# Gated cross-attention with a sign-weight FFN on one core: the first stage with x loaded from ScalarE's queue, weights alone in SyncE's and rounded one unit ahead

## The reference

```python
x = x + tanh(g_xattn) * attention(layernorm(x), ctx, ctx, mask, wq, wk, wv, wo)
x = x + tanh(g_ffn) * ffn(layernorm(x), weight, bias, gate_w, in_channel_scale, out_channel_scale)
```

## Time and profile before

| | us |
|---|---|
| median of three runs | 1526.08 |
| lowest and highest | 1522.46, 1531.22 |
| the profiled execution | 1529.2 |
| its span | 1527.4 |
| first matmul of the first stage | 14.40 |
| first matmul of the next stage | 90.44 |

### The profile page before, as it was taken

One profiled execution on the slowest core, in us unless ns is written; L12 is line 12 of the kernel. 1 busy time (PEld: TensorE's weight loads), 2 busy tenths in 40 slices (PEclk: granted clock), 3 DMA queues, 4 the chain that ended last, 5 costly groups with the idle time before them and its releaser, 6 DMA issues.

```text
span 1527.4 us, 26067 instructions
## 1 busy us (share of the span) xinstructions
PE 1483.2 (97%) x8720; PEld 1311.3 (86%) x8720; DVE 1031.4 (68%) x2373; ACT 615.2 (40%) x1183; POOL 722.8 (47%) x594
## 2 busy tenths in 40 slices
PE   5989999999999999999999998999999999989998
PEld 5878888888888888888888788999999999978887
DVE  5837888888778888888788874455455455765653
ACT  5732222222222222222222364556567565634442
POOL 6834445654555546555455452333333333335554
PEclk9999999999999999999999999999999999999999
DMA  7830222212221222212221686443997442542311
GB/s 271 289 110 27 71 77 69 69 48 69 76 76 48 76 69 76 69 41 76 73 79 42 194 332 219 133 130 100 374 392 226 132 131 96 187 144 106 110 69 69
DMA packets 95210, 192.56 MB, mean 126 GB/s; under 512 B 9056, under 2 KB 36192, under 8 KB 95008
## 3 DMA queue, kind: packets, MB, share of 16 engines
q1 hardware_dynamic: 88944, 179.74, 36.2%
q10 hardware_dynamic: 6192, 11.86, 2.3%
HBM read 133.90 MB, written 57.67 MB: 125 GB/s over the span
## 4 chain that ended last, share of the span: by engine, by line
PE 85%; issue 3%; POOL 2%; DVE 2%; DMA 1%; ACT 1%; SPq 0%; POOLq 0%; ACTq 0%; DVEq 0%
PE bank L52 19%; PE bank L53 19%; PE bank L54 19%; PE bank L915 7%; PE bank L914 7%; PE bank L916 7%; PE bank L937 5%; POOL last_rows L1352 1%; DMA w_raw<-in_wo 1%; PE bank L950 1%; DVE project L1504 1%; ACT project L1130 1%; POOL feed L1344 0%; PE bank L959 0%; PE bank L982 0%
## 5 line engine op out<-in xcount | busy, mean ns | idle before, releaser
L52 PE MATMUL bank<-x_hi,w_hi 128*128 128x512 f32 x1024 | 399.2, 390 | 3.9 <-PEq L67 3.9
L53 PE MATMUL bank<-x_lo,w_hi 128*128 128x512 f32 x1024 | 398.9, 390 | 0.0
L54 PE MATMUL bank<-x_hi,w_lo 128*128 128x512 f32 x1024 | 398.8, 389 | 0.0
L1504 DVE TENSOR_TENSOR project<-bank,project 64x256 fp32r<-64x256 f32 x512 | 216.1, 422 | 197.4 <-ACT project L1130 192.0
L1357 POOL TENSOR_TENSOR w_lo<-w_raw,w_hi 128x512 fp32r<-128x512 f32 x128 | 165.7, 1296 | 285.7 <-ACT w_hi L1122 285.7
L1130 ACT CAST project<-bank 64x256 fp32r<-64x256 f32 x512 | 188.4, 368 | 160.6 <-PE bank L54 150.6
L1291 POOL TENSOR_TENSOR q_lo<-rot,q_hi 128x512 fp32r<-128x512 f32 x128 | 164.9, 1293 | 184.7 <-ACT q_hi L1061 184.6
L915 PE MATMUL bank<-project,project 128*128 128x256 f32 x832 | 235.8, 283 | 0.0
L914 PE MATMUL bank<-project,project 128*128 128x256 f32 x832 | 235.8, 283 | 0.0
L916 PE MATMUL bank<-project,project 128*128 128x256 f32 x832 | 235.8, 283 | 0.0
L52 PEld LDWEIGHTS bank<-x_hi,w_hi 128*128 128x128 f32 x1024 | 192.6, 188 | 44.2 <-issue 4.1
(11 more groups left out here) (143 smaller groups left out, 2696.7 us busy)
## 6 DMA issues: line engine op xcount, KB each, us to landing
w_raw<-in_wo SPq DMA_DIRECT2D x128, 256.0 KB, 3.0
project<-probs_scratch SPq DMA_DIRECT2D x52, 512.0 KB, 8.7
w_raw<-in_wq SPq DMA_DIRECT2D x32, 512.0 KB, 5.3
probs_scratch<-pt_hi SPq DMA_DIRECT2D x64, 256.0 KB, 2.6
probs_scratch<-pt_lo SPq DMA_DIRECT2D x64, 256.0 KB, 3.2
x_in<-in_x SPq DMA_DIRECT2D x16, 512.0 KB, 4.9
last_rows<-in_x SPq DMA_DIRECT2D x8, 1024.0 KB, 6.2
x_scratch<-last_rows SPq DMA_DIRECT2D x8, 1024.0 KB, 5.6
```

Source lines behind the costliest of these rows:

```text
L52: pe.matmul(out, hi, rhs_hi, start=first, stop=False, **kw)
L53: pe.matmul(out, hi, rhs_lo, start=False, stop=False, **kw)
L54: return pe.matmul(out, lo, rhs_hi, start=False, stop=last, **kw)
L1504: done = nc.vector.tensor_tensor(vw_lo[i][at], vw_ps[hp % VW_BANKS][b * SK:(b + 1) * SK, h, :], vw_hi[i][at].bitcast(F32), ALU.subtract)
```

## The change

Five edits, all in `prepare`:

1. SyncE loads both halves of ctx and units 0 and 1 first, and then tiles 0 to 2 of x. The later tiles are loaded from ScalarE's queue, each right behind the normalisation that frees its buffer.
2. SyncE's queue then holds only the weights and, in ScalarE's place, the stores of keys and values: from step 6 every second step behind the load of a unit, from step 14 each step.
3. ScalarE rounds unit `n + 1` in step `n`. Unit 0 is rounded between the two halves of ctx.
4. GpSimd takes the deviation of tile `n` behind the low part of unit `n` (tiles 0 and 1 both behind unit 1).
5. VectorE takes ctx_lo before the statistics of tile 0.

The waits for the last stores stand on SyncE instead of ScalarE.

```diff
@@ sync
-            def load_x(i):
-                wait(sp, xn_ready, i - XB + 1)
-                sp.dma_start(x_in[:, i % XB], a["x"][i * P:(i + 1) * P, :]).then_inc(x_in_sem[i % XB], 16)
+            def store_keys(gp):
...
+            def store_values(g):
...
             for h in range(2):
                 src = a["ctx_t"].rearrange("(k p) t -> p k t", p=P)[:, half(h)]
                 sp.dma_start(ctx_raw[:, half(h)], src).then_inc(ctx_in[h], 16)
-                if h == 0:
-                    load_unit(0)
-                    load_x(0)
-            load_unit(1)
-            load_x(1)
-            load_x(2)
+                load_unit(h)
+            for i in range(XB):
+                sp.dma_start(x_in[:, i], a["x"][i * P:(i + 1) * P, :]).then_inc(x_in_sem[i], 16)
             for n in range(2, UNITS):
                 load_unit(n)
-                if n + 1 < NLN:
-                    load_x(n + 1)
+                if n >= KEYS_AT and n % 2 == 0 and (n - KEYS_AT) // 2 < GP:
+                    store_keys((n - KEYS_AT) // 2)
+                if n >= VALUES_AT:
+                    store_values(n - VALUES_AT)
+            for g in range(UNITS - VALUES_AT, HKV):
+                store_values(g)
@@ scalar
+            def load_x(i):
+                act.wait_ge(xn_ready, i - XB + 1)
+                act.dma_start(x_in[:, i % XB], a["x"][i * P:(i + 1) * P, :]).then_inc(x_in_sem[i % XB], 16)
...
                 nc.scalar.copy(ctx_hi[:, half(h)], ctx_raw[:, half(h)]).then_inc(ctx_hi_ready, 1)
+                if h == 0:
+                    split_unit(0)
             for n in range(NU + 2):
-                split_unit(n)
+                if n + 1 < UNITS:
+                    split_unit(n + 1)
                 if n < NLN:
                     normalise(n)
+                if n + XB < NLN:
+                    load_x(n + XB)
                 if HKV <= n - 1 < NU:
                     value_high(n - 1 - HKV)
                 if n >= 2:
                     turned(n - 2)
-
-                if 0 <= n - 2 < HKV and (n - 2) % 2 == 1:
-                    store_keys((n - 2) // 2)
-                if n - 2 >= HKV:
-                    store_values(n - 2 - HKV)
@@ gpsimd
-            reciprocal_deviation(0)
             for n in range(UNITS):
...
-                if n + 1 < NLN:
-                    reciprocal_deviation(n + 1)
+                if n == 1:
+                    reciprocal_deviation(0)
+                if 1 <= n < NLN:
+                    reciprocal_deviation(n)
@@ vector
-            statistics(0)
             for h in range(2):
                 dve.wait_ge(ctx_hi_ready, h + 1)
                 nc.vector.tensor_tensor(ctx_lo[:, half(h)], ctx_raw[:, half(h)], ctx_hi[:, half(h)].bitcast(F32),
                                         ALU.subtract).then_inc(ctx_lo_ready, 1)
+            statistics(0)
```

More of the change, by code:

```diff
@@ L66, in prepare @@
     XB = 3
+    KEYS_AT, VALUES_AT = 6, HKV + 6
     with ExitStack() as ctx:
@@ L141, in load_unit @@
                 sp.dma_start(raw(n), a["wkv"][n] if n < NU else a["wq"][0, n - NU]).then_inc(w_in[n % 4], 16)
-            def load_x(i):
-                wait(sp, xn_ready, i - XB + 1)
-                sp.dma_start(x_in[:, i % XB], a["x"][i * P:(i + 1) * P, :]).then_inc(x_in_sem[i % XB], 16)
+            def store_keys(gp):
+                sp.wait_ge(k_roped, gp + 1)
+                for c in range(2):
+                    sp.dma_start(scratch["keys"][c, gp * P:(gp + 1) * P, :], k_rot[:, 2 * c, :]).then_inc(k_stored, 16)
+            def store_values(g):
+                sp.wait_ge(v_lo_ready, g + 1)
+                for c, part in enumerate((v_hi, v_lo)):
+                    sp.dma_start(scratch["values"][c, g], part[:, g % 2].bitcast(F32)).then_inc(v_stored[g % 2], 16)
             for h in range(2):
@@ L149, in _ @@
                 sp.dma_start(ctx_raw[:, half(h)], src).then_inc(ctx_in[h], 16)
-                if h == 0:
-                    load_unit(0)
-                    load_x(0)
-            load_unit(1)
-            load_x(1)
-            load_x(2)
+                load_unit(h)
+            for i in range(XB):
+                sp.dma_start(x_in[:, i], a["x"][i * P:(i + 1) * P, :]).then_inc(x_in_sem[i], 16)
             for n in range(2, UNITS):
                 load_unit(n)
-                if n + 1 < NLN:
-                    load_x(n + 1)
+                if n >= KEYS_AT and n % 2 == 0 and (n - KEYS_AT) // 2 < GP:
[4 more added lines that the diff above has]
+                store_values(g)
+            sp.wait_ge(k_stored, 32 * GP)
+            for i in range(2):
+                sp.wait_ge(v_stored[i], 32 * HKV // 2)
         @block.tensor
@@ L215, in turned @@
                 last.then_inc(x_hi_ready, 1)
[L217 to L225, removed]
             act.dma_start(ident[:], a["ident"]).then_inc(ident_in, 16)
@@ L240, in _ @@
                     turned(n - 2)
-                if 0 <= n - 2 < HKV and (n - 2) % 2 == 1:
-                    store_keys((n - 2) // 2)
-                if n - 2 >= HKV:
-                    store_values(n - 2 - HKV)
-            act.wait_ge(k_stored, 32 * GP)
-            for i in range(2):
-                act.wait_ge(v_stored[i], 32 * HKV // 2)
         @block.gpsimd
```

## The result

| | before | changed kernel |
|---|---|---|
| median of 6 runs | 1526.62 us | 1518.19 us |
| lowest and highest | 1522.46, 1531.22 | 1515.49, 1518.85 |
| ratio | | 0.9936, 95% interval 0.9917 to 0.9954 |
| profiled execution, its span | 1529.2, 1527.4 | 1515.49, 1513.7 |
| next stage's first matmul | 90.44 | 80.01 |

The medians differ by 8.4 us; the ratio, which is not formed from these two medians, is worth 9.8, with 7.0 to 12.7 as its interval. The forecast 14.5 (a ratio of 0.9905) lies outside it: the sign was right, and the measured gain is a third smaller than the forecast one. The next stage starts at 80.01; a start "after 80 us" was the prediction's own sign of being wrong, so it is met, by a hundredth.

The account below looks back on a forecast made before the run. The first stage was bound by a ring in which ScalarE's normalisations waited for TensorE's transposes. Gains 5.4 + 4.0 + 2.9 + 1.4 + 0.8 = 14.5 took the median 1526.1 to 1511.6 us, range 1506.5 to 1519.

Parts of the forecast that it names:

- The start: First stage up to its first matmul: reordered loads and casts let TensorE start at 9.0 instead of 14.40, 5.4 us gained.
- The next units: Units 2 to 4: late tile 0 of x costs 0.7 us at unit 2; unit 3 at 21.9, unit 4 at 25.7.
- The pace: Units 0 to 14: the ring no longer bounds, TensorE's 3.76 us plus 1.0 in all; 55.3 instead of 59.27, 4.0 gained.
- The stores: Value stores on SyncE's queue have two turns, some 7 us, to land before v_hi needs the buffer at unit 15.
- Unit 15: Unit 15 follows 3.76 us behind unit 14 instead of 6.66 if value stores land in time: 2.9 gained.
- its clock: With no pause before unit 15 the clock stays up: its matmuls take 2.94 us instead of 4.31, 1.4 gained.
- The tail: From the last matmul to the next stage: unit 17's rounding done a turn earlier, 5.0 us instead of 5.8, 0.8 gained.
- Rival 2: ScalarE becomes the pace if the x load costs it 1.1 us: 4.3 and 4.5 per unit, 1517.6 us; chance 0.12.
- Rival 1: DMA engines become the pace at 305 GB/s: units 2 to 14 gain 2.6 us less, 1514.2 us; chance 0.14.
- The signs: First matmul near 9, unit gaps 3.7 to 3.9, no pause at unit 15, next stage near 76; wrong if after 80.
- the missing ring: Sign in the first stage: ScalarE waits for transposes, 13.3 us before, not above a microsecond in all after unit 4.
- Against the median: Whole kernel: 14.5 off the profiled 1529.2 gives 1514.7; that execution lies 3.1 above the median 1526.1, so 1511.6 us.

Follow-up runs that it names:

- all three edits: Changed kernel with four v buffers, four x buffers and ScalarE's x load behind the x_hi casts: 1514.34 us once, then median 1514.53 us, ratio to before 0.9902.

## Why the prediction was right in sign and too large

- **The start** (5.4): measured 5.25. The queue order, the casts and GpSimd's place came out as worked out; w_lo began at 7.74 and the first matmul at 9.15. The first unit ran slowly as forecast, its matmuls 0.21 apart instead of 0.12. The granted clock that the trace shows for it (9 to 15 us) is 1.00, so that the 1.2 GHz level was the reason is not shown. ctx_lo beside w_lo took 1.48 where a half had taken 1.2.
- **The next units** (0.7 lost at unit 2): the loss was 0.64 larger by unit 4, in two pieces. 0.37 were there at unit 2 (9.47 behind unit 0 instead of 9.1): w_lo of unit 1 took 2.94 beside ctx_lo where the earlier trace rows has 2.52, and the deviation, the normalisation and the rounding of unit 2 stand behind it. For this contention the prediction says "I put nothing down". The other 0.27 came by unit 4. The step that failed is "From unit 3 on ScalarE is a turn ahead: unit 3 at 21.9, unit 4 at 25.7". It followed ScalarE and left out VectorE's wait for tile 3 of x, whose buffer the first normalisation releases: 4.16 idle at 20.49, then the first rotation and x_lo in one row, and tile 2's transposes 0.20 late. With the fourth x buffer unit 4 came at 26.08 and 25.91 instead of 26.49.
- **The pace**: VectorE's 3.9 and "buffers let TensorE hide about half: 1.0" gave 1.0 for units 4 to 12, and 1.03 was measured; half the rotation took it away. That the sums agree is luck, for the split was another: nothing was hidden in the key units (3.93 each, 0.68 for units 4 to 8), another 0.35 came behind the last rotation (x_lo of tile 6, 0.21 at 49.28), and ScalarE's 0.2 per value unit did not show in units 10 to 12 (3.75 each).
- **The stores.** What failed is "If they land in that", some 7 us. Landings of values took up to 7.1 us, beside weights and x, and held v_hi up by 1.54 and 0.94; 1.65 of it reached TensorE. Four buffers took 1.6 back. The time left was also shorter than 7: the first v_lo was ready at 51.1 and its buffer wanted at 57.1. For the second the issue itself was late, at 56.08 where v_lo was ready at 54.4, behind the load of a unit and an issue of v_hi that took 1.21. The condition was named and no price was put on it: the landings of 512 KB loads had a longest of 9.6, so a miss was to be expected for some of the stores.
- **Unit 15** (2.9) **and its clock** (1.4): both as forecast. No pause, granted clock 1.00 from 60 to 70 and 0.99 from 70 to 80, 2.95 for 24 matmuls instead of 4.31.
- **The tail** (0.8 gained, measured 0.75 lost): the step "Unit 17's rounding ... is done a turn earlier". In the order of the code it is, but ScalarE was a turn late: L208 at 74.57 and v_hi at 75.61 stand between x_hi of tiles 13 and 14, and 6.55 passes instead of 5.0. Neither the changed kernel's waits for stores (6.55 without them) nor the rotation (6.53) are its cause. It was 5.83 and 6.04 where TensorE had lost 3 us earlier, so that ScalarE caught up, and 5.68 and 6.28 with all three edits, but 8.22 with the later load alone. The short ones fit an engine whose turn in the last units is 3.4 even without a load (its normalisations start at 65.40 and 68.79), close to TensorE's 3.74, so that a lag is made up by 0.35 a turn; but no run has tested it alone: what sets the tail between 5.7 and 8.2 stays open.
- **Rival 2**: the gap behind a normalisation was 0.41, with the 0.1 of overlap lost 0.5, near the 0.54 taken. It did not bound the key units (the later load gained 0.26 in units 4 to 12); in the run without rounding ahead it lay in the ring. Its 1517.6 is the number nearest the median, but its signs, ScalarE without idle time and TensorE waiting for w_lo, did not come. **Rival 1** priced its loss at 2.6; units 2 to 14 took 48.15, which is 1.95 more than the forecast 46.2, but at waits for x_lo and for stores, not at the weights. Whether full DMA engines made the stores late is not shown.
- **The signs**: the first matmul, the missing ring and unit 15 came as named. The gaps between units were to be 3.7 to 3.9 and ran from 3.74 to 4.72, and the next stage was to start near 76.
- **Against the median**: the stage's 10.4 off 1526.6 gives 1516.2; 1518.19 was measured, and the 2.0 between lie within the interval of the ratio.

## To carry over

When one ring is opened, walk the next candidates with their waits, not only with their busy time: here a late third tile of x and a stretched low part at the start (0.64), a store that must land within two turns (1.65) and an engine that is one turn late at the end (1.55) took nearly all of the 4.1 us that were missing from 14.5. A queue move is judged by what stands behind its waits: the three runs with one part of the change undone gave up 9.25 to 14.7 us where the whole had gained 10.4. Where the schedule is tight, look for instructions of VectorE with two operands in SBUF that lie beside GpSimd's within a fraction of a microsecond: a harmless edit can push them onto each other.

## What the runs showed of the hardware

- VectorE against GpSimd: a 128x256 operation with both operands in SBUF took 0.42 alone and more in eight of the runs where a w_lo was under way: 0.69 to 0.87 (the versions with a fourth buffer of x, and the two orders of VectorE), 1.08 (stores back in ScalarE's queue) and 1.46 to 1.52 where a half of w_lo had just started (also all four rotations with x back in SyncE's queue). Wherever it started, it ended 0.23 to 0.29 behind the running half of w_lo (1.29 long), as if it had to wait for it. The 128x1024 ctx_lo went from 1.22 to 1.48. The Trainium skill, "GPSIMD Engine Reference", section Key points, names this contention; the trace agrees, and the price on a short instruction was up to a factor of 3.6.
- The landing of a 128 KB store differed much from kernel to kernel, and not by its queue alone (least, median, most). Values from SyncE's queue: 1.7 / 3.5 / 7.1 in the changed kernel, 1.7 / 1.8 / 4.4 with x back in that queue. Values from ScalarE's: 1.7 / 2.0 / 6.3 before the change, 1.7 / 1.9 / 5.4 with the stores back there. Keys: 2.0 / 2.2 / 2.6 from SyncE's in the changed kernel, 3.9 / 5.2 / 6.0 from ScalarE's with the stores back there. The kernels differ in their loads at that time too; what makes a store late is not shown.
